# A selective scan whose last state column is copied by another engine

## The chip, the cores and the metric

The kernel runs on one core of one Trainium2 chip. The metric is the device time in microseconds of one execution; the time before is the median of three runs.

## The reference

A decoder layer over 4 sequences of 1024 tokens, width 512: a Mamba block, cross-attention to 64 context rows, a mixture-of-experts projection with low-rank experts, and a layer norm after each. What matters here is the scan of the Mamba block (d_inner 1024, 16 states):

```python
dA = jnp.exp(jnp.einsum('bld,dn->bldn', dt, A))
dBu = jnp.einsum('bld,bln,bld->bldn', dt, Bm, u_act)
def step(h, inputs):
    dA_t, dBu_t = inputs
    h = dA_t * h + dBu_t
    return (h, h)
_, hs = lax.scan(step, h0, (dA.transpose(1, 0, 2, 3), dBu.transpose(1, 0, 2, 3)))
y = jnp.einsum('lbdn,bln->bld', hs, Cm) + u_act * Dp
y = y * jax.nn.silu(z)
```

The block's output goes through a SwiGLU of width 2048. Cross-attention has 16 heads of 32, with a temperature for each head out of a small network that reads statistics of the scores.

## The kernel before

The work is cut into 8 chunks of 512 tokens; chunks 2b and 2b+1 are the halves of sequence b. An even chunk starts its scans from zero, an odd one from the state that the even one left. Channels lie on the 128 partitions, so 1024 channels make 8 blocks, taken in 4 pairs. One step of the scan is one pair and one of the 16 states over 512 tokens: 64 steps a chunk, 512 in all.

A step goes through three engines. GpSimd multiplies dt*u by the row of B (`times_b`, L1070) into one of three buffers `hb`. ScalarE makes the two decays with Exp into two PSUM banks (`decays`, L1127). VectorE runs two `tensor_tensor_scan` in place in `hb` (L1425), each of which frees its decay bank. GpSimd multiplies `hb` in place by the row of C (`times_c`, L1080). VectorE adds it to the sum in PSUM (L1435), which frees the buffer. GpSimd does the product by B of the next step ahead of the product by C of this one (AHEAD = 1), so its order is B(g+1), C(g), B(g+2), C(g+1). ScalarE's decays of step g+1 go into the banks that the scans of step g free.

In even chunks the last column of `hb` after the scan is the state that the odd chunk begins with. As the product by C overwrites `hb`, ScalarE first copies the two values of each partition into `state` (L1195), after the decays of the next step in its queue, and the product by C waits for it through the semaphore `st_saved` (L1078). In odd chunks there is neither copy nor wait. The odd chunk's first scan waits for all copies of its even chunk (L1419).

All the rest is dense work: the front of a chunk (norm, input projection, convolution; stream f), output projection (f), SwiGLU, norm, query (stream y), the statistics of attention (s), attention and experts (x, and w for the last chunk), the gates z and the softplus of dt (l). It's worked on beside the scan by TensorE, ScalarE and VectorE. The scan is stream m. The residual adds of GpSimd are L1100 and L1103, its product dt*u once per pair is L1090.

Every engine executes a list in fixed order. The lists come out of `schedule()`, a planner that runs when the kernel is built: `parts(u)` gives for each unit its costs by engine and what it waits for, and at each point an engine takes from the streams the unit that can begin first, with `LOOK` as a tolerance by stream; among units that are equally early the lower key wins. Stream m has key 0, l has 1; for the others the key is chunk + PHASE + (share done) / WORK. A unit that is late in reality holds up everything behind it in its engine's list. SyncE issues all loads in an order that follows the planned times too (`loads()`).

Of the kernel before, what the change touches and what calls it, by code (L numbers as in the profile page):

```python
# [7 lines left out]
BATCH, SEQ, DM, DI, NS, DTR, DFF = 4, 1024, 512, 1024, 16, 32, 2048  # L8
# [3 lines left out]
CH = 512  # L12
# [11 lines left out]
HB, AHEAD, BC = 3, 1, 2  # L24
# [7 lines left out]
PE, ACT_, DVE, POOL = "PE", "ACT", "DVE", "POOL"  # L32
# [22 lines left out]
def pair_of(n):  # L55
    return divmod(n, PAIRS)


def step_of(g):
    return divmod(g, STEPS)  # L60
# [104 lines left out]
def parts(u):  # L165


    kind, c, key = u[0], u[1], u[1:]
    i = u[2] if len(u) > 2 else None
    b, last, got = c // 2, TT - 1, []  # L170

    def part(eng, us, *after, takes=(), gives=(), name=None):
        got.append((eng, us, after, name, takes, gives))
# [25 lines left out]
    elif kind == "step":  # L199
        g, total = c * STEPS + i, CHUNKS * STEPS  # L200
# [3 lines left out]
        for n in (0, 1) if g == 0 else (g + 1,) if g + 1 < total else ():  # L204
            at = step_of(n)
            for jj in range(2):
                part(ACT_, 0.68, ("scan", *step_of(n - 1), jj), ("sp4", at[0], 2 * (at[1] // NS) + 1), name=("exp", *at, jj))
        if c % 2 == 0:
            part(ACT_, 0.2, ("scan", c, i, 1), name=("saved", c, i))
        if i % NS == 0:  # L210
            part(ACT_, 1.4, ("gate", *pair_of(g // NS - 1)), name=("yp", c, i // NS))
        for jj in range(2):
            part(DVE, 1.25, ("s1", c, i), ("exp", c, i, jj), name=("scan", c, i, jj))
        part(POOL, 2.35, ("scan", c, i, 1), ("saved", c, i), name=("s3", c, i))
    elif kind == "sum":
        part(DVE, 1.3, ("s3", c, i), ("yp", c, i // NS))
    elif kind == "gate":
# [143 lines left out]


SCAN_BANKS, DENSE_BANKS = (0, 1, 2, 3), (4, 5, 6, 7)
WORK = {"x": 1534.0, "w": 127.4, "s": 422.9, "y": 661.5, "f": 650.3}
PHASE = {
# [5 lines left out]
}  # L371


# [83 lines left out]
def schedule():  # L457
# [9 lines left out]
    for name, units in streams.items():  # L467
        for u in units:
            got = parts(u)
            todo[u] = len(got)  # L470
            pending.add(u)
            share[name] = share.get(name, {})
            share[name][u[1]] = share[name].get(u[1], 0.0) + sum(p[1] for p in got)
            key = 0 if name == "m" else 1 if name == "l" else u[1] + PHASE[name][u[1]] + share[name][u[1]] / WORK[name]
            by_eng = {}
            for n, p in enumerate(got):
                by_eng.setdefault(p[0], []).append((n, p))
                pending.add((u, n))
                if p[3]:
                    pending.add(p[3])  # L480
            for e, ps_ in by_eng.items():
                queue[e][name].append((u, ps_, key))
# [25 lines left out]
    while True:  # L508
        best = None
        for e in queue:  # L510
            names = (inside[e],) if inside[e] else streams
            mine = None
            for name in names:
                t = ready(e, name)
                if t is not None:
                    rank = (max(t, at[e] + LOOK[name]), queue[e][name][place[e][name][0]][2])
                    if mine is None or rank < mine[0]:
# [41 lines left out]
    return streams["m"], begun, {u: v[0] for u, v in done.items()}, order, taken  # L559


LOOK = {"m": 0.379, "l": 0.018, "x": 0.019, "w": 0.041, "s": 0.247, "y": 0.171, "f": 0.0}
MIXER, BEGUN, DONE, ORDER, DENSE_TAKES = schedule()


# [85 lines left out]
def decoder_layer(nc, A, out):  # L651
    f32 = mybir.dt.float32
    ALU = mybir.AluOpType
    ACT = mybir.ActivationFunctionType
    AX = mybir.AxisListType.X
    ctx = ExitStack()
    with ctx:
        def sb(name, shape):
            return ctx.enter_context(nc.sbuf_tensor(name, shape, f32))
# [43 lines left out]
        hb = sb("hb", [P, HB, 2, CH])  # L703
# [5 lines left out]
        state = sb("state", [P, JB, NS])  # L709
# [99 lines left out]
        s = type("Sems", (), S)  # L809
# [8 lines left out]
        def filled(eng, key):  # L818

            bank, n = USE[key]  # L820
            eng.wait_ge(full[bank], n + 1)
            return ps[:, bank]
# [21 lines left out]
        def emptied(eng, key):  # L844

            bank, n = USE[key]
            eng.wait_ge(free[bank], n + 1)
# [32 lines left out]
        def firsts_done(eng, n):  # L880

            at_least(eng, s.s1_ready, n)

        def summed(eng, n):

            eng.wait_ge(s.sum_done, n + 1)
# [162 lines left out]
        @block.gpsimd  # L1049
        def _(pool):  # L1050
            nc.gpsimd.memset(kbd[:, :, :, :], 0.0).then_inc(s.zeroed, 1)
            nc.gpsimd.memset(vbd[:, :, :], 0.0).then_inc(s.zeroed, 1)
            nc.gpsimd.memset(sta[:, :, :], 0.0).then_inc(s.zeroed, 1)
            nc.gpsimd.memset(eps_t[:, :], EPS).then_inc(s.zeroed, 1)
            nc.gpsimd.memset(ones_t[:, :], 1.0).then_inc(s.zeroed, 1)
            nc.gpsimd.memset(negs_t[:, :], -1.0).then_inc(s.zeroed, 1)
            nc.gpsimd.memset(zero3[:, :], 0.0).then_inc(s.zeroed, 1)
            nc.gpsimd.memset(t_w2[:, HID:P], 0.0).then_inc(s.zeroed, 1)

            TTn = nc.gpsimd.tensor_tensor  # L1060

            def times_b(n):
                c, k = step_of(n)
                if k % NS == 0:
                    pool.wait_ge(s.dtu_ready, n // NS + 1)
                pool.wait_ge(b_in[n % BC], 16 * (n // BC + 1))

                if n >= HB:
                    summed(pool, n - HB)
                TTn(hb[:, n % HB], dtu[:, :, :], bc[:, 0, n % BC].unsqueeze(1).broadcast_to([P, 2, CH]), ALU.mult  # L1070
                    ).then_inc(s.s1_ready, 1)

            def times_c(n):
                c, k = step_of(n)
                emptied(pool, ("da", c, k, 0))
                emptied(pool, ("da", c, k, 1))
                if c % 2 == 0:
                    pool.wait_ge(s.st_saved, (c // 2) * STEPS + k + 1)  # L1078
                pool.wait_ge(c_in[n % BC], 16 * (n // BC + 1))
                TTn(hb[:, n % HB], hb[:, n % HB], bc[:, 1, n % BC].unsqueeze(1).broadcast_to([P, 2, CH]), ALU.mult  # L1080
                    ).then_inc(s.s3_done, 1)

            for unit in ORDER[POOL]:
                kind, c = unit[0], unit[1]
                i = unit[2] if len(unit) > 2 else None
                if kind == "du":
                    emptied(pool, ("dt", c, 2 * i))
                    emptied(pool, ("dt", c, 2 * i + 1))
                    firsts_done(pool, c * STEPS + i * NS)
                    TTn(dtu[:, :, :], dt[:, i % 2], u[:, c % 2, 2 * i:2 * i + 2], ALU.mult).then_inc(s.dtu_ready, 1)  # L1090
                elif kind == "step":
                    g = c * STEPS + i
                    for n in range(AHEAD + 1) if g == 0 else (g + AHEAD,) if g + AHEAD < CHUNKS * STEPS else ():
                        times_b(n)
                    times_c(g)
                elif kind == "bo":
                    pool.wait_ge(s.const_in, 16 * CONSTS)
                    for c4 in range(KC):
                        filled(pool, ("tr", c, 0, c4))
                    TTn(res[:, c % 3, i], res[:, c % 3, i], bo_b[:, :], ALU.add).then_inc(s.bo_in, 1)  # L1100
                elif kind == "out":
                    emptied(pool, ("out", c, i))
                    TTn(res[:, c % 3, i], ht[:, i], res[:, c % 3, i], ALU.add).then_inc(s.res_in, 1)  # L1103
# [3 lines left out]
        def _(act):  # L1107
            A_ = nc.scalar.activation
# [20 lines left out]
            for unit in ORDER[ACT_]:  # L1129
                kind, c = unit[0], unit[1]  # L1130
                i = unit[2] if len(unit) > 2 else None
                b, half = divmod(c, 2)
# [36 lines left out]
                elif kind == "sp1":  # L1169
# [4 lines left out]
                    elif c or i:  # L1174
                        n, p = pair_of(c * PAIRS + i // 2 - 1)
# [10 lines left out]
                elif kind == "step":  # L1186
                    g = c * STEPS + i
                    for n in (0, 1) if g == 0 else (g + 1,) if g + 1 < CHUNKS * STEPS else ():
                        decays(*step_of(n))
                    p, n = divmod(i, NS)  # L1190
                    if half == 0:

                        emptied(act, ("da", c, i, 0))
                        emptied(act, ("da", c, i, 1))
                        A_(state[:, 2 * p:2 * p + 2, n], hb[:, g % HB, :, CH - 1], ACT.Copy).then_inc(s.st_saved, 1)  # L1195
                    if n == 0:
                        for jj in range(2):
                            key = ("yp", c, p, jj)
# [78 lines left out]
                elif kind == "e1":  # L1277
# [4 lines left out]
                    if wide1(c):  # L1282
                        n = 2 * i + hf
# [83 lines left out]
        def _(dve):  # L1367
# [14 lines left out]
            for unit in ORDER[DVE]:  # L1382
# [113 lines left out]
                elif kind in ("rstd", "xrstd"):  # L1496
# [3 lines left out]
                    else:  # L1500
                        dve.wait_ge(s.ln_sd, c + 1)
                    _, mean_var, sd = norm_of(x, c)
                    ch.link(V.reciprocal(sd[:, 1, :], sd[:, 0, :]))
                    V.scalar_tensor_tensor(sd[:, 2, :], mean_var[:, :, 0], -1.0, sd[:, 1, :], ALU.mult, ALU.mult
# [430 lines left out]
```

## Time and profile before

| what | value |
|---|---|
| median of three runs | 3673.43 us (3672.25 to 3678.02) |
| the profiled execution | 3670.03 us, span 3668.2 us |
| TensorE matmul busy | 3004.8 us, 82% |
| VectorE busy | 2788.1 us, 76% |
| GpSimd busy | 2532.7 us, 69% |
| ScalarE busy | 2141.0 us, 58% |
| chain that ended last | TensorE 18% of the span, VectorE 2%, ScalarE 2%, issue 1% |
| mean granted TensorE clock | 0.905 |

The span runs from the first to the last instruction. The chain that ended last is followed back from the end through what released each instruction; the shares named cover less than a quarter of the span. A wait is put down to the instruction that released it last. An engine's list can't be overtaken, so a wait at its head delays all that is behind it.

### The profile page before, as it was taken

The numbers are of one execution on the slowest core, as the hardware profiler recorded it, in microseconds if no ns is written. First come the engines' busy times: TensorE is split into PE (matmuls) and PEld (weight loads), VectorE is DVE, ScalarE is ACT, GpSimd is POOL, SyncE is SP. The second block draws the span as 40 slices with busy tenths as digits, with TensorE's granted clock in tenths as the row PEclk, the third lists the DMA queues.
The fourth block names the chain that finished last, engine by engine and source line by source line (L and its number), as shares of the span: only waits on it lengthen the run. The fifth ranks groups of instructions, "written<-read, shape, count | busy, mean of one in ns | idle before, by whom it ended". The sixth has DMA issues, their size and how long they took to land. (4 is left out here: it accounts for less than half of the span.)

```text
span 3668.2 us, 32780 instructions
## 1 busy us (share of the span) xinstructions
PE 3004.8 (82%) x8248; PEld 1452.7 (40%) x8248; DVE 2788.1 (76%) x3376; ACT 2141.0 (58%) x4823; POOL 2532.7 (69%) x1132
## 2 busy tenths in 40 slices
PE   6711389867986899899996899999998799999868
PEld 3200134333433444444443344444443344554444
DVE  3878889988888798879897788877898898322353
ACT  5544475567556775777558675667557756441332
POOL 0699969987988598876987677776798798300000
PEclk8855699978997999999997999999999799999979
DMA  4433445544554444554642444453555354212100
GB/s 158 122 115 127 147 142 192 171 137 153 177 169 124 133 150 141 174 166 133 203 167 93 154 135 141 157 172 135 159 175 170 123 175 143 101 42 88 39 1 23
DMA packets 225430, 497.91 MB, mean 136 GB/s; under 512 B 32348, under 2 KB 32732, under 8 KB 224988
## 3 DMA queue, kind: packets, MB, share of 16 engines
q1 hardware_dynamic: 225244, 495.82, 41.7%
q8 instruction: 70, 1.15, 0.1%
q14 instruction: 116, 0.95, 0.1%
HBM read 485.76 MB, written 9.96 MB: 135 GB/s over the span
## 5 line engine op out<-in xcount | busy, mean ns | idle before, releaser
L1080 POOL TENSOR_TENSOR hb<-hb,bc 128x1024 f32<-128x1024 f32 x512 | 1206.2, 2356 | 436.2 <-ACT state L1195 219.1
L1070 POOL TENSOR_TENSOR hb<-dtu,bc 128x1024 f32<-128x1024 f32 x512 | 1206.5, 2356 | 111.8 <-DVE ps L1435 107.0
L1127 ACT ACTIVATE ps<-dt,a_neg 128x512 f32<-128x512 f32 x1024 | 691.5, 690 | 687.2 <-DVE hb L1425 685.0
L1651 PE MATMUL ps<-fT,wden 128*128 128x512 f32 x2304 | 1036.2, 605 | 52.5 <-DVE dt L1413 7.5
L1425 DVE TENSOR_TENSOR_SCAN hb<-ps,hb 128x512 f32<-128x512 f32 x512 | 596.7, 1207 | 108.9 <-POOL hb L1070 96.6
L1651 PEld LDWEIGHTS ps<-fT,wden 128*128 128x128 f32 x2304 | 439.8, 194 | 600.1 <-issue 593.1
L1425 DVE TENSOR_TENSOR_SCAN hb<-ps,state,hb 128x512 f32<-128x512 f32 x512 | 627.2, 1266 | 65.5 <-POOL hb L1070 41.7
L1435 DVE TENSOR_TENSOR ps<-ps,hb 128x1024 f32<-128x1024 f32 x512 | 624.3, 1219 | 12.2 <-POOL hb L1080 11.8
L1651 PE MATMUL ps<-xnT,wmix 128*128 128x512 f32 x1024 | 456.7, 601 | 126.0 <-DMA wmix<-in_w_mix 113.4
L1741 PE MATMUL ps<-wden,hm 128*128 128x512 f32 x1024 | 456.2, 597 | 28.8 <-DVE res L1481 12.4
L1702 PE MATMUL ps<-wmix,u 128*128 128x512 f32 x512 | 241.2, 626 | 147.5 <-issue 82.0
L1651 PEld LDWEIGHTS ps<-xnT,wmix 128*128 128x128 f32 x1024 | 196.4, 193 | 374.9 <-issue 258.7
L1741 PEld LDWEIGHTS ps<-wden,hm 128*128 128x128 f32 x1024 | 191.8, 191 | 272.2 <-issue 224.9
L1702 PEld LDWEIGHTS ps<-wmix,u 128*128 128x128 f32 x512 | 100.7, 201 | 281.8 <-issue 209.2
L1100 POOL TENSOR_TENSOR res<-res,bo_b 128x512 f32<-128x512 f32 x32 | 39.8, 1276 | 243.5 <-PE ps L1754 243.5
L1777 PE MATMUL ps<-kbd,qT 128*128 128x256 f32 x512 | 150.0, 435 | 64.5 <-DVE se L1523 44.6
L1239 ACT ACTIVATE hm<-ps 128x512 f32<-128x512 f32 x128 | 76.2, 596 | 215.7 <-PE ps L1651 130.4
L1481 DVE TENSOR_TENSOR res<-ps,res 128x512 f32<-128x512 f32 x128 | 87.5, 683 | 112.8 <-PE ps L1741 112.4
L1393 DVE SCALAR_TENSOR_TENSOR ps<-stage,cols,ps 128x512 f32<-128x512 f32 x192 | 144.6, 753 | 32.0 <-ACT ps L1157 27.4
L1342 ACT ACTIVATE xw<-ps,nm,ftv 128x64 f32<-128x64 f32 x384 | 149.4, 416 | 6.0 <-PE ps L1777 5.8
L1465 DVE SCALAR_TENSOR_TENSOR hm<-hm,ps 128x512 f32<-128x512 f32 x128 | 86.8, 678 | 84.4 <-ACT hm L1239 83.6
L1777 PEld LDWEIGHTS ps<-kbd,qT 128*128 128x128 f32 x512 | 104.2, 215 | 105.7 <-DVE se L1523 54.5
(242 smaller groups left out, 3504.5 us busy)
## 6 DMA issues: line engine op xcount, KB each, us to landing
bc<-bc_dram SPq DMA_DIRECT2D x1024, 256.0 KB, 3.3
wden<-in_w SPq DMA_DIRECT2D x192, 512.0 KB, 3.9
wmix<-in_w_mix SPq DMA_DIRECT2D x128, 512.0 KB, 3.9
watt<-in_w_qof SPq DMA_DIRECT2D x26, 512.0 KB, 4.1
stage<-in_x SPq DMA_DIRECT2D x8, 1024.0 KB, 5.8
res<-in_x SPq DMA_DIRECT2D x8, 1024.0 KB, 6.6
wden<-in_w_qof SPq DMA_DIRECT2D x16, 512.0 KB, 4.2
out<-res SPq DMA_DIRECT2D x8, 1024.0 KB, 5.0
```

Of the source, the lines that this page charges most:

```text
L1070: TTn(hb[:, n % HB], dtu[:, :, :], bc[:, 0, n % BC].unsqueeze(1).broadcast_to([P, 2, CH]), ALU.mult).then_inc(s.s1_ready, 1)
L1080: TTn(hb[:, n % HB], hb[:, n % HB], bc[:, 1, n % BC].unsqueeze(1).broadcast_to([P, 2, CH]), ALU.mult).then_inc(s.s3_done, 1)
L1127: A_(dst, dt[:, p % 2, jj], ACT.Exp, scale=a_neg[:, j, n:n + 1]).then_inc(full_of(key), 1)
L1342: ins = A_(eb_of(c)[:, hh], bank[:, h], ACT.Exp, bias=nm2[:, TT * half + i, hh:hh + 1], scale=ftv[:, 0, hh:hh + 1], accum_out=den_of(c)[:, ...
L1393: ins = V.scalar_tensor_tensor(acc, up[:, i % 2, tap:tap + CH], conv_w[:, i, tap:tap + 1], acc, ALU.mult, ALU.add)
L1425: V.tensor_tensor_scan(hb[:, n % HB, jj], src, hb[:, n % HB, jj], first, ALU.mult, ALU.add).then_inc(free_of(key), 1)
L1435: V.tensor_tensor(ps[:, 2:4], ps[:, 2:4], hb[:, n % HB], ALU.add).then_inc(s.sum_done, 1)
L1481: V.tensor_tensor(res[:, c % 3, tt], src, res[:, c % 3, tt], ALU.add).then_inc(free_of(key), 1)
L1651: ins = M(dst, a, b, start=start and n == 0, stop=stop and n == len(pairs) - 1)
L1702: ins = M(ps[:, USE[key][0]], u[:, half, j, t * P:(t + 1) * P], wo[:, j % 2], start=j == 0, stop=j == JB - 1)
L1741: ins = M(dst, hm[:, f, tt * P:(tt + 1) * P], wi[:, (f % 2) * 512:(f % 2) * 512 + 512], start=f == 0, stop=f == FG - 1)
L1777: ins = M(dst[:, m * 256:(m + 1) * 256], qT[:, c4, T * P:(T + 1) * P], kbd[:, b % 2, c4], start=True, stop=True)
```

## The change

GpSimd copies the last column itself, right before the product by C in its own list, and then waits for its own copy by the same semaphore. ScalarE's copy is gone, with its two waits. In the planner the part of 0.2 on ScalarE is gone, the product by C costs 0.15 more in even chunks and no longer waits for the copy. All the constants of the planner's priorities, WORK, PHASE and LOOK, have other values, so that the order of the lists of all engines, and the order of the loads, may be another.

```diff
@@ parts(u), kind == "step"
-        if c % 2 == 0:
-            part(ACT_, 0.2, ("scan", c, i, 1), name=("saved", c, i))
...
-        part(POOL, 2.35, ("scan", c, i, 1), ("saved", c, i), name=("s3", c, i))
+        part(POOL, 2.35 + (0.15 if c % 2 == 0 else 0.0), ("scan", c, i, 1), name=("s3", c, i))
@@ planner constants
-WORK = {"x": 1534.0, "w": 127.4, "s": 422.9, "y": 661.5, "f": 650.3}
+WORK = {"x": 169.8, "w": 831.5, "s": 26.2, "y": 31.4, "f": 43.7}
 PHASE = {
-    "x": (34.753, 4.637, 32.716, 36.312, 63.287, 39.291, 57.599, 95.752),
-    "w": (12.607, 28.312, 24.365, -32.043, -13.09, 0.11, 30.675, 18.153),
-    "s": (0.314, -8.39, 7.942, 5.462, -10.774, -24.164, -52.826, -0.355),
-    "y": (38.588, 1.209, -24.936, -33.417, -23.064, -23.341, -23.392, -15.228),
-    "f": (15.256, -7.945, 2.695, 24.097, -13.326, -28.258, 38.233, -20.089),
+    "x": (36.744, 5.957, 40.05, 35.575, 68.382, 58.488, 60.427, 102.854),
+    "w": (7.884, 22.737, 33.738, -18.942, -11.063, 11.758, 36.876, 33.748),
+    "s": (8.781, -11.538, 8.696, -0.908, -19.87, -28.791, -53.763, -10.604),
+    "y": (47.653, 15.941, -14.86, -35.472, -20.046, -26.021, -8.484, 1.026),
+    "f": (20.176, 0.519, 12.645, 36.762, 1.801, -21.137, 44.543, -11.967),
 }
-LOOK = {"m": 0.379, "l": 0.018, "x": 0.019, "w": 0.041, "s": 0.247, "y": 0.171, "f": 0.0}
+LOOK = {"m": 0.384, "l": 0.043, "x": 0.022, "w": 0.044, "s": 0.245, "y": 0.237, "f": 0.0}
@@ GpSimd, times_c(n)
                 if c % 2 == 0:
+                    p, m = divmod(k, NS)
+                    nc.gpsimd.tensor_copy(state[:, 2 * p:2 * p + 2, m], hb[:, n % HB, :, CH - 1]).then_inc(s.st_saved, 1)
                     pool.wait_ge(s.st_saved, (c // 2) * STEPS + k + 1)
@@ ScalarE, kind == "step"
-                    if half == 0:
-
-                        emptied(act, ("da", c, i, 0))
-                        emptied(act, ("da", c, i, 1))
-                        A_(state[:, 2 * p:2 * p + 2, n], hb[:, g % HB, :, CH - 1], ACT.Copy).then_inc(s.st_saved, 1)
```

## Rows read from the trace of the kernel before

**Rows 1.** Busy us by stretch after the scan: PE, PEld, DVE, ACT, POOL, clock, DMA

```profile
3158.00:3450.00 292.00, 284.07 (x818) 141.48 (x816) 69.71 (x146) 93.24 (x297) 5.00 (x4) 0.98 0.23 78
```

**Rows 2.** The same view, chunks 0, 2, 4 and 6

```profile
98.90:434.00 335.10, 96.01 (x200) 37.56 (x198) 270.79 (x266) 167.38 (x297) 306.25 (x133) 0.64 0.39 121
795.00:1167.00 372.00, 312.57 (x735) 141.33 (x735) 319.80 (x350) 232.41 (x529) 315.73 (x140) 0.90 0.49 157
1560.00:1956.00 396.00, 371.86 (x978) 175.65 (x976) 332.94 (x409) 257.57 (x567) 321.26 (x145) 0.97 0.48 159
2370.00:2789.00 419.00, 385.51 (x1005) 181.50 (x1005) 343.29 (x418) 261.56 (x582) 316.76 (x143) 0.96 0.47 154
```

**Rows 3.** Chunk 0, one line's instructions and their waits: L1080, then L1425's wait

```profile
L1080 POOL TENSOR_TENSOR hb<-hb,bc x65: 2329/2347/2391, 98.9 to 432.4; 128x1024 f32<-128x1024 f32 x65
...
  ACT state L1195: 23.9, 5
...
  POOL hb L1070: 55.1, 47
```

**Rows 4.** L1080 in chunks 2 to 6: ns min/median/max, first, last start; waits: us, times

```profile
L1080 POOL TENSOR_TENSOR hb<-hb,bc x64: 2336/2354/2386, 799.8 to 1165.2; 128x1024 f32<-128x1024 f32 x64
...
  ACT state L1195: 33.5, 21
...
L1080 POOL TENSOR_TENSOR hb<-hb,bc x65: 2346/2356/2384, 1165.2 to 1558.1; 128x1024 f32<-128x1024 f32 x65
...
  issue: 63.4, 11
...
L1080 POOL TENSOR_TENSOR hb<-hb,bc x65: 2344/2355/2382, 1558.1 to 1954.4; 128x1024 f32<-128x1024 f32 x65
...
  ACT state L1195: 66.3, 24
...
L1080 POOL TENSOR_TENSOR hb<-hb,bc x65: 2334/2356/2400, 1954.4 to 2368.2; 128x1024 f32<-128x1024 f32 x65
...
L1080 POOL TENSOR_TENSOR hb<-hb,bc x64: 2340/2355/2377, 2368.2 to 2782.4; 128x1024 f32<-128x1024 f32 x64
...
  ACT state L1195: 95.4, 25
```

**Rows 5.** Timeline, a step of chunk 3: start us, us, what [idle before, releaser]

```profile
1235.66 2.46 DVE L1425 TENSOR_TENSOR_SCAN hb<-ps,state,hb 128x512 f32<-128x512 f32 x2
...
1238.25 2.36 POOL L1080 TENSOR_TENSOR hb<-hb,bc 128x1024 f32<-128x1024 f32 x1 [19.86 <-issue]
```

**Rows 6.** Timeline, a step of chunk 6 with a long wait

```profile
2526.97 2.34 DVE L1425 TENSOR_TENSOR_SCAN hb<-ps,hb 128x512 f32<-128x512 f32 x2 [1.64 <-ACT ps L1127]
...
2543.94 1.30 ACT L1127 ACTIVATE ps<-dt,a_neg 128x512 f32<-128x512 f32 x2
2545.16 0.20 ACT L1195 ACTIVATE state<-hb 128x2 f32<-128x2 f32 x1
...
2545.59 2.36 POOL L1080 TENSOR_TENSOR hb<-hb,bc 128x1024 f32<-128x1024 f32 x1 [13.09 <-ACT state L1195]
```

**Rows 7.** GpSimd: the timeline round L1090, and two groups (busy us, mean ns)

```profile
192.33 2.35 POOL L1080 TENSOR_TENSOR hb<-hb,bc 128x1024 f32<-128x1024 f32 x1
194.63 2.34 POOL L1090 TENSOR_TENSOR dtu<-dt,u 128x1024 f32<-128x1024 f32 x1
197.05 2.34 POOL L1070 TENSOR_TENSOR hb<-dtu,bc 128x1024 f32<-128x1024 f32 x1
...
L1057 POOL MEMSET zero<- 128x3 f32 x1 | 0.1, 101 | 0.0
...
L1100 POOL TENSOR_TENSOR res<-res,bo_b 128x512 f32<-128x512 f32 x32 | 39.8, 1276 | 243.5 <-PE ps L1754 243.5
```

**Rows 8.** Groups of VectorE: the scan with and without a carried state

```profile
L1425 DVE TENSOR_TENSOR_SCAN hb<-ps,hb 128x512 f32<-128x512 f32 x512 | 596.7, 1207 | 108.9 <-POOL hb L1070 96.6
L1425 DVE TENSOR_TENSOR_SCAN hb<-ps,state,hb 128x512 f32<-128x512 f32 x512 | 627.2, 1266 | 65.5 <-POOL hb L1070 41.7
```

## The prediction

> **What bounds the kernel now.** I read four views in this order: the chain that ended last (its shares stand in the table above, most of it TensorE's), busy time by stretch, the two GpSimd products by stretch, and single steps of the timeline. A step is one (pair, state) of the scan: GpSimd multiplies by B (L1070), ScalarE makes two exponentials (L1127), VectorE scans twice (L1425), GpSimd multiplies by C (L1080), VectorE adds (L1435). There are 512, 64 to a chunk, eight chunks. From 3158 us on GpSimd works 5 of 292 us, so the scan is over, while TensorE works 284 of them [rows 1]; with a span of 3668.2 us, some 510 us of dense work follow the scan. The end therefore moves only if the dense work starts sooner, which the scan governs, or if TensorE's idle time inside the scan shrinks.
>
> That idle time is 59 us of 372 in chunk 2, 24 of 396 in chunk 4, 33 of 419 in chunk 6, and 239 of 335 in chunk 0 [rows 2]. In chunk 0 there is no dense work yet, so whatever lengthens chunk 0 delays the first dense unit one for one. GpSimd is busy 306 of 335 us there, and VectorE waited 47 times, 55.1 us, for the product by B; GpSimd waited only 5 times, 23.9 us, for the copy [rows 2, 3]. So chunk 0 is paced by GpSimd. In chunks 2, 4 and 6 GpSimd waited for the copy 21, 24 and 25 times, 33.5, 66.3 and 95.4 us [rows 4]. That makes 70 of 192 steps and 195 us: the prize on the label.
>
> **How much of such a wait is the copy.** In an undisturbed odd step, where nothing is copied, the product by C starts 0.13 us after the second scan ends (1235.66 + 2.46 = 1238.12, then 1238.25) [rows 5]. In an even step two exponentials of the next step, which wait for the same scans, and then the copy stand in between: the second exponential takes 0.65 us (half of the 1.30 of two) and the copy 0.20, and with a hand-over like the odd step's 0.13 us once more about 0.95 us is lost against the odd step [rows 5, 6]. Long waits are of another kind. The longest shown, 13.09 us, has its scans over at 2529.31; ScalarE was in dense units ahead of this step and reached the copy at 2545.16 [rows 6]. After the change GpSimd would go on at about 2532.5, where it fell idle. But the next scans need exponentials from the same late ScalarE, so GpSimd does one product and the one by B behind it and then stands before the next product by C. What it gains is the product it has already done, at most 2.36 us, and not 13.
>
> **Part 1, the copy goes to GpSimd: its price.** It is paid in 256 steps. The trace has no GpSimd copy. Below, the nearest row is a memset of 128x3, 0.101 us; above, the fixed part of a two-input product, 2 x 1.276 - 2.355 = 0.197 us from its widths of 512 and 1024 [rows 4, 7]. To it comes the wait for its own semaphore (the new wait stays, now behind GpSimd's own copy). This one is in the trace: dtu's product is followed by the first product by B, which waits for it, and that starts at 197.05, 2.42 us after 194.63, where independent neighbours start 2.30 us apart (192.33 and 194.63) [rows 7]. That is 0.12 us. With 0.10 and 0.19 for the copy itself this makes 0.22 and 0.31. Behind the waiting product are queued the next product by B and the residual adds; VectorE waits for both. I take 0.25, nearer to the small memset, as two elements a partition are moved. It can't be nothing or a gain: it is one more instruction in a queue that starts each when the one before is nearly done.
>
> The Trainium skill (GPSIMD Engine Reference, the note that consecutive Pool instructions are not a barrier between Q7 cores) says that completion gates whatever waits on the semaphore, not the next instruction. This fits: 0.12 us more with a wait than without [rows 7]; by the page alone there is no figure for the sum.
>
> **Chunk 0.** 59 steps without a copy wait pay 0.25 us each, +15 us. The 5 that waited save 0.95 each, -5 us. Net +10 us, on the path because GpSimd paces the chunk and TensorE has nothing else; ends +8 (0.22) and +18 (0.31 and no saving, if those waits are the start-up's). The cover would be GpSimd's own idle time in the chunk, 335 - 306 = 29 us, 24 of which are these five waits, so there is hardly any.
>
> **Chunks 2, 4 and 6.** 70 waits, each worth 0.95 (the lag alone) to 2.36 us (one product). Most of the waits are short, so 1.2 is taken: 84 us. Price 192 x 0.25 = 48 us. Net 36 us of GpSimd's time. How much reaches the end? A control lies in the same trace: chunks 3 and 5 have the wait-free form throughout. From first to last product by C a step took 5.80 us in chunk 2 (365.4 over 63), 6.14 in chunk 3 (392.9 over 64), 6.19 in chunk 4 (396.3 over 64), 6.47 in chunk 5 (413.8 over 64) and 6.57 in chunk 6 (414.2 over 63) [rows 4]. Each odd chunk lies between its neighbours: 6.14 against their mean 6.00, and 6.47 against 6.38. The scans with a carried state cost 1.266 us in place of 1.207, 0.12 us a step [rows 8]; without it the odd ones would be at 6.02 and 6.35. So a chunk without the copy wait is no faster than one with it: in chunk 3 GpSimd stood 63.4 us in 11 waits before the product by C all the same [rows 4]. This speaks for a share near zero. On the other side, the odd chunks carry other dense units than the even ones, and TensorE still has 116 us idle in the three even chunks to take. Between these two I take a third: -12 us. Ends: 0, and two thirds, -24 us, with the waits at 1.2; at 2.36 each and all of it, 165 - 48 = 117 us, just TensorE's idle time, which no row makes likely.
>
> **Part 2, ScalarE loses 256 copies** of 0.20 us [rows 6]. Its dense units in even chunks start that much sooner: 192 x 0.20 = 38 us in chunks 2, 4 and 6, of which again only what was late counts. A quarter, -9 us; ends 0 and half, -18. In chunk 0 ScalarE has room, so nothing there.
>
> **Part 3, the planner.** It decides each engine's order, and with the step's costs (0.2 on ScalarE gone, 0.15 more on GpSimd, under my 0.25) all of its priorities change. A lower key goes first: chunk number plus PHASE, and over the chunk the share of its work by WORK. In chunk 3 the four dense streams y, s, f, x stood at -30.4, 8.5, 27.1 and 39.3 and stand at -32.5, 2.1, 39.8 and 38.6; in chunk 4 s moves ahead of f (-6.8 and -9.3 before, -15.9 and 5.8 after), in chunk 2 too; in chunk 1 y falls behind x. Most ranks stay, so most of the order should. The trace can't price another order. The nearest row is one stall that comes or goes with a unit's place, the 13.09 us of [rows 6]. I put it at zero, with ends of -20 and +20, one or two such stalls net.
>
> **Sum.** +10 - 12 - 9 + 0 = -11 us. The profiled execution took 3670.03 us (span 3668.2 and 1.8 around it), which gives 3659; the median of the three runs is 3.4 us above it, so against the median it is 3673.4 - 11 = 3662 us, 0.3% faster. A measurement of this kernel tells about 0.2% (7 us) from no change.
>
> **Rivals.** *Covered*: the share is zero as chunks 3 and 5 say, and ScalarE's relief is given back at the next dense wait. Then +10 and a few us of ScalarE's relief: 3673 to 3680, taken at 3676. For it: the step times of [rows 4]. Against: 70 waits that do vanish.
>
> *GpSimd becomes the bound (slower)*: the place is the row of products in even chunks. 122 steps of chunks 2, 4 and 6 did not wait for the copy and gain nothing; at 0.31 and half of them on VectorE's path they cost 122 x 0.31 / 2 = 19 us, with chunk 0 at +18, and the waits that go are replaced by waits for ScalarE's exponentials: 3673 + 37 = 3710, or 3673 + 15 + 10 = 3698 at 0.25. It decides from a price of 0.34 us a copy with the shares above (59 p - 5 + (192 p - 84) / 3 - 9 = 0), and at 0.25 as soon as ScalarE's relief is lost and under 10 / 36 of the net gain in the later chunks gets through. Against: VectorE waited for GpSimd's products by B in chunk 0 mostly [rows 3]. The Trainium skill (Perfetto Trace Analysis, Identifying the Most-Contended Engine) would have the engine with the highest occupancy relieved first; moving work from ScalarE (257.6 of 396 us in chunk 4) to GpSimd (321.3) goes the other way [rows 2], and by it this rival would hold.
>
> *The order*: the new sequence puts a dense unit that is late ahead of an exponential. One or two stalls of 13 us more: 3685 to 3695. The reverse, with two fewer and the whole two thirds: 3673 + 10 - 24 - 18 - 10 = 3631.
>
> **Chances.** Forecast 0.38 (3645 to 3666), the strong gain 0.07, covered 0.28, GpSimd's price 0.15, a worse order 0.12. Faster 0.44, same 0.27 (most of covered and the edge of the forecast), slower 0.29. The range takes in the strong gain's end and the slower rivals but for the last: 3630 to 3702.
>
> **What would show it.** The copy on GpSimd lasts 0.10 to 0.19 us and the product by C starts at least 0.22 us after the copy's start. In chunk 0 the step goes from near 5.2 to near 5.4 us and the next chunk's first product is 7 to 18 us later. GpSimd waits before the product by C in chunks 2, 4 and 6 fall from 195 us, but those named by VectorE's scans take much of their place; the steps there are 0.0 to 0.15 us shorter. The prediction is wrong if chunk 0 isn't longer, if a copy costs over 0.31 us, or if the chunks 4 and 6 change by more than 20 us each: then the order, and not the wait, made the result.

## The result

The changed kernel took 3693.4 us (median of four, 3687.05 to 3696.16) against 3672.84 us (median of four) for the kernel before: a ratio of 1.0052, 95% interval 1.0034 to 1.0069. It is some 19 us slower, where 11 us faster had been forecast. The time lies inside the range, on the other side of no change.

The profiled execution has a span of 3685.3 us. Busy time by stretch, chunks 0, 2, 4 and 6 of the kernel after, cut at the first product by C of each chunk (columns as in [rows 1]):

```profile
97.00:440.00 343.00, 93.08 (x192) 36.74 (x192) 271.02 (x263) 158.30 (x230) 315.47 (x197) 0.63 0.38 118
...
800.00:1169.00 369.00, 302.86 (x721) 137.59 (x720) 317.13 (x347) 224.74 (x450) 326.45 (x204) 0.90 0.51 158
...
1581.00:1984.00 403.00, 363.69 (x923) 169.49 (x921) 340.68 (x412) 252.61 (x517) 331.78 (x209) 0.94 0.49 158
...
2413.00:2782.00 369.00, 342.45 (x825) 152.51 (x824) 323.40 (x383) 219.88 (x405) 327.32 (x206) 0.97 0.52 167
```

Against [rows 2], GpSimd has 9 to 11 us more work in each and ScalarE less. Chunk 6 is some 55 us shorter and chunk 4 is 7 us longer (table below): that is no matter of a copy. The copy's own instructions and their waits in the kernel after, in chunks 2, 4 and 6 (they answer to the waits of [rows 4]):

```profile
L1077 POOL COPY state<-hb x63: 177/187/213, 804.5 to 1164.0; 128x2 f32<-128x2 f32 x63
...
  DVE hb L1420: 19.5, 7
...
  DVE hb L1420: 47.9, 14
...
  DVE hb L1420: 14.4, 5
```

The 195 us of waits for ScalarE's copy in these chunks are gone; 82 us of waits for the scans stand in their place. With the order of before (e1 below) it is 11.0 + 42.7 + 64.2 = 118 us.

How long each chunk lasts, in the profiled executions, from its first product by C to that of the next one, and the tail (us, worked out from first starts; chunk 7 lasts to the end of its last product by C, and the tail begins there). The experiments' names are explained below. Each row is a single execution and can lie up to 7 us from its kernel's median (e4: 3668.9 against 3676.1). Chunk 1 lies between 359.0 and 361.4 in all fourteen kernels, so 2 us in one chunk mean nothing by themselves.

| kernel | 0 | 1 | 2 | 3 | 4 | 5 | 6 | 7 | tail |
|---|---|---|---|---|---|---|---|---|---|
| before | 333.5 | 360.3 | 372.6 | 392.8 | 396.3 | 413.8 | 423.7 | 364.3 | 512.0 |
| after | 342.5 | 359.8 | 369.0 | 412.5 | 403.3 | 429.0 | 368.1 | 392.8 | 510.7 |
| e1, move only | 347.0 | 359.0 | 367.4 | 393.4 | 394.5 | 419.2 | 420.6 | 364.4 | 512.0 |
| e2, order only | 328.8 | 361.4 | 373.1 | 409.9 | 411.7 | 434.6 | 372.4 | 391.3 | 514.8 |
| e3, no copy, old order | 330.5 | 359.0 | 363.0 | 389.7 | 391.2 | 416.7 | 418.7 | 366.3 | 515.4 |
| e4, no copy, new order | 328.8 | 359.7 | 361.9 | 409.8 | 405.5 | 430.3 | 367.0 | 393.3 | 513.7 |

After has e1's longer chunk 0 and e2's pattern from chunk 3 on. So there are two parts, and they can be taken apart.

### The profile page after: what moved, and what is told of

Its sections match the earlier page's. It is cut to its first block, busy times and chain, and to the rows that moved or that the text cites. A ratio compares the mean times of both kernels' runs of the same rounds, so it can differ in the third digit from the quotient of the medians.

```text
span 3685.3 us, 32529 instructions
## 1 busy us (share of the span) xinstructions
PE 2989.2 (81%) x8248; PEld 1445.0 (39%) x8248; DVE 2791.8 (76%) x3376; ACT 2117.2 (57%) x4573; POOL 2575.0 (70%) x1388
## 3 DMA queue, kind: packets, MB, share of 16 engines
q1 hardware_dynamic: 225244, 495.82, 41.8%
## 4 chain that ended last, share of the span: by engine, by line
PE 58%; POOL 12%; ACT 11%; DVE 11%; issue 6%; DMA 1%; SPq 1%; POOLq 0%; DVEq 0%; ACTq 0%
PE ps L1646 39%; PE ps L1736 10%; POOL hb L1068 6%; POOL hb L1080 5%; DVE hb L1420 4%; ACT ps L1298 2%; PE ps L1697 2%; PE ps L1679 1%; PE ps L1772 1%; DVE ps L1430 1%; ACT xw L1337 1%; PE ps L1807 1%; ACT ps L1127 1%; PE ps L1840 1%; PE ps L1853 1%
## 5 line engine op out<-in xcount | busy, mean ns | idle before, releaser
L1080 POOL TENSOR_TENSOR hb<-hb,bc 128x1024 f32<-128x1024 f32 x512 | 1205.2, 2354 | 285.5 <-issue 251.1
L1420 DVE TENSOR_TENSOR_SCAN hb<-ps,hb 128x512 f32<-128x512 f32 x512 | 597.1, 1208 | 107.8 <-POOL hb L1068 101.1
L1090 POOL TENSOR_TENSOR dtu<-dt,u 128x1024 f32<-128x1024 f32 x32 | 75.3, 2354 | 94.6 <-DVE dt L1408 86.7
## 6 DMA issues: line engine op xcount, KB each, us to landing
wden<-in_w SPq DMA_DIRECT2D x192, 512.0 KB, 4.0
wmix<-in_w_mix SPq DMA_DIRECT2D x128, 512.0 KB, 4.1
watt<-in_w_qof SPq DMA_DIRECT2D x26, 512.0 KB, 4.5
wden<-in_w_qof SPq DMA_DIRECT2D x16, 512.0 KB, 4.2
```

The costliest lines, as they stand in the source:

```text
L1420: V.tensor_tensor_scan(hb[:, n % HB, jj], src, hb[:, n % HB, jj], first, ALU.mult, ALU.add).then_inc(free_of(key), 1)
```

## The experiments

All ratios are to the kernel before, run on the same chip beside them.

### The two parts of the change, one at a time

**e1** moves the copy and leaves the planner as it was:

```diff
+                    nc.gpsimd.tensor_copy(state[:, 2 * p:2 * p + 2, m], hb[:, n % HB, :, CH - 1]).then_inc(s.st_saved, 1)
...
-                        A_(state[:, 2 * p:2 * p + 2, n], hb[:, g % HB, :, CH - 1], ACT.Copy).then_inc(s.st_saved, 1)
```

> The copy goes to GpSimd and nothing else: every engine's order and the order of the loads are those of the kernel before. Theory A (the new order makes most of the loss): chunk 0 grows by 9 us as it did in the changed kernel (333.5 to 342.5 us from its first product by C to that of chunk 1), and later chunks give a part back, so 3672 to 3680 us. Theory B (the copy's price of 0.25 us on GpSimd makes the loss, in all 256 steps): 3688 to 3697 us, like the changed kernel.

Measured: 3675.96 us, ratio 1.0005 (0.9993 to 1.0017).

**e2** is the kernel after with those lines put back as they were: all planner constants and costs are the new ones, ScalarE copies.

> The order of the changed kernel on every engine, but ScalarE copies and GpSimd waits for it, as before. Theory A: 3680 to 3690 us, as chunks 3, 5 and 7 stay longer by the new order. Theory B: 3670 to 3677 us, no slower than the kernel before.

Measured: 3695.77 us, ratio 1.0068 (1.0050 to 1.0086), above both bands. Theory A holds, with a larger size than it gave: the new order alone is 23 us slower, and the move alone is within a few us of nothing on either order (+3.4 on the old one, 3693.4 - 3695.8 = -2.4 on the new one).

### What copy and wait are worth together

**e3** and **e4** have neither copy nor wait, in the old and the new order:

```diff
-                if c % 2 == 0:
-                    pool.wait_ge(s.st_saved, (c // 2) * STEPS + k + 1)
...
-                    if half and i == 0:
-                        dve.wait_ge(s.st_saved, (b + 1) * STEPS)
```

> The order of before, with no copy and no wait for one at all: the state that an odd chunk starts from is left at zero, so that part of the computation is left out. This is the most that taking the wait away can bring. If the wait is covered by late dense work, as chunks 3 and 5 of the kernel before suggested: 3665 to 3673 us. If 70 waits of about a microsecond reach the end by a third, as predicted: 3645 to 3660 us.

> The order of the changed kernel, with no copy and no wait (the carried state is left out and is zero). Against the changed kernel (3693 us) it leaves out only the 256 copies of 0.25 us on GpSimd. Theory A: 9 us less in chunk 0 and little elsewhere, 3680 to 3686 us. Theory B: 3670 us or less.

Measured: e3 3658.28 us, in the band of the predicted third, ratio 0.9962 (0.9947 to 0.9977); e4 3676.09 us, 1.0005 (0.9993 to 1.0017). So ScalarE's copy and the wait for it cost 14 us in the old order, and GpSimd's copy costs 17.7 us there (3675.96 - 3658.28) and 17.3 us in the new one (3693.4 - 3676.1). In the new order ScalarE's copy and wait cost 19.7 us (3695.8 - 3676.1). So the move is about even: it takes away 14 to 20 us and puts 17 to 18 in their place. e4 came in below what theory A expected, since GpSimd's copy costs 13.7 us in chunk 0 and not 9 (the new order by itself begins with a chunk 0 of 328.8 us), and is paid outside chunk 0 as well: 7.1 us of chunk 2 in the new order, 4.4 in the old. And e4 is slower than e3 by 17.8 us with no copy in either: the order's loss doesn't hang on the copy.

### The price of a GpSimd copy

The timeline of GpSimd in chunk 0 of the kernel after:

```profile
301.82 2.36 POOL L1068 TENSOR_TENSOR hb<-dtu,bc 128x1024 f32<-128x1024 f32 x1
304.12 0.18 POOL L1077 COPY state<-hb 128x2 f32<-128x2 f32 x1
304.39 2.35 POOL L1080 TENSOR_TENSOR hb<-hb,bc 128x1024 f32<-128x1024 f32 x1
306.70 2.34 POOL L1068 TENSOR_TENSOR hb<-dtu,bc 128x1024 f32<-128x1024 f32 x1
308.99 0.18 POOL L1077 COPY state<-hb 128x2 f32<-128x2 f32 x1
```

A step takes 308.99 - 304.12 = 4.87 us, where two products took 2 x 2.30 = 4.60 before [rows 7]: the price is 0.27 us, and in chunk 0 GpSimd has little idle time to hide it (e1: 18.5 us in 5 waits for the scans). **e6** doubles it, with a second copy and a second wait:

```diff
+                    nc.gpsimd.tensor_copy(state[:, 2 * p:2 * p + 2, m], hb[:, n % HB, :, CH - 1]).then_inc(s.st_saved, 1)
+                    pool.wait_ge(s.st_saved, 2 * ((c // 2) * STEPS + k) + 1)
```

> Order of before, copy on GpSimd, but done twice in each even step, each with its wait, so the price doubles from 0.25 to 0.5 us. If chunk 0 is bound by GpSimd, it grows by 64 x 0.25 = 16 us once more, from 347 to 363 us. If a GpSimd copy costs nothing behind dense work, the later chunks stay and the time is 3676 + 16 = 3692 us; if its price reaches the end by a third in chunks 2, 4 and 6 too, 192 x 0.25 / 3 = 16 us more, 3708 us.

Measured: 3709.07 us, ratio 1.0097 (1.0082 to 1.0112). The first product by C of chunk 0 and that of chunk 1, in e1 and then in e6:

```profile
L1082 POOL TENSOR_TENSOR hb<-hb,bc x65: 2337/2342/2362, 100.1 to 447.1; 128x1024 f32<-128x1024 f32 x65
```

```profile
L1084 POOL TENSOR_TENSOR hb<-hb,bc x65: 2340/2343/2368, 97.4 to 456.9; 128x1024 f32<-128x1024 f32 x65
```

347.0 and 359.5 us: +12.5 in chunk 0 (16 had been expected). Chunks 2, 4 and 6 grew by 9.6, 5.5 and 1.8 us, 17 of 192 x 0.25 = 48 us, so about a third of the price stays there. GpSimd is the bound in chunk 0, where 0.20 of 0.25 us a step come through. In the later chunks less comes through, and the less the busier TensorE is (308, 367 and 387 us in chunks 2, 4 and 6 of e1); that the one is the reason of the other isn't shown.

**e5** leaves chunk 0 with ScalarE and gives chunks 2, 4 and 6 to GpSimd:

```diff
                 if c % 2 == 0:
+                    if c:
+                        p, m = divmod(k, NS)
+                        nc.gpsimd.tensor_copy(state[:, 2 * p:2 * p + 2, m], hb[:, n % HB, :, CH - 1]).then_inc(s.st_saved, 1)
...
-                    if half == 0:
+                    if c == 0:
```

> Order of before. ScalarE copies in chunk 0, GpSimd in chunks 2, 4 and 6. The copy alone moved everywhere gave 3676 us. If its price is paid in chunk 0 alone (13 us there) and the later even chunks gain what they showed (5, 2 and 3 us shorter): 3660 to 3666 us. If the later chunks' gain was only the start-up's delay given back: 3671 to 3677 us.

Measured: 3665.41 us, ratio 0.9978 (0.9969 to 0.9987). Chunk 0 lasts 335.2 us, chunks 2, 4 and 6 last 368.3, 394.5 and 420.6: the gain in the later chunks is their own, 9 us over the three.

### Why long waits gave so little

The same stall in chunk 6, in the kernel before ([rows 6] shows its beginning) and in e1. GpSimd in the kernel before, and ScalarE's next exponentials:

```profile
2551.59 2.35 POOL L1080 TENSOR_TENSOR hb<-hb,bc 128x1024 f32<-128x1024 f32 x1 [1.34 <-ACT state L1195]
...
2556.22 2.35 POOL L1080 TENSOR_TENSOR hb<-hb,bc 128x1024 f32<-128x1024 f32 x1
...
2560.84 2.35 POOL L1080 TENSOR_TENSOR hb<-hb,bc 128x1024 f32<-128x1024 f32 x1
...
2557.76 0.69 ACT L1127 ACTIVATE ps<-dt,a_neg 128x512 f32<-128x512 f32 x1 [3.24 <-DVE hb L1425]
```

And in e1:

```profile
2541.77 2.36 POOL L1082 TENSOR_TENSOR hb<-hb,bc 128x1024 f32<-128x1024 f32 x1
2544.08 2.35 POOL L1070 TENSOR_TENSOR hb<-dtu,bc 128x1024 f32<-128x1024 f32 x1
2559.70 0.19 POOL L1079 COPY state<-hb 128x2 f32<-128x2 f32 x1 [13.27 <-DVE hb L1422]
2559.96 2.35 POOL L1082 TENSOR_TENSOR hb<-hb,bc 128x1024 f32<-128x1024 f32 x1
...
2565.44 2.36 POOL L1082 TENSOR_TENSOR hb<-hb,bc 128x1024 f32<-128x1024 f32 x1
...
2571.21 2.35 POOL L1082 TENSOR_TENSOR hb<-hb,bc 128x1024 f32<-128x1024 f32 x1
...
2555.91 1.29 ACT L1129 ACTIVATE ps<-dt,a_neg 128x512 f32<-128x512 f32 x2
...
2569.73 0.69 ACT L1129 ACTIVATE ps<-dt,a_neg 128x512 f32<-128x512 f32 x1 [3.36 <-DVE hb L1422]
```

Put e1's times back by 11.97 us, by which its ScalarE is later at this place (2555.91 against 2543.94 in [rows 6]). Four products by C in a row then start at 2529.80, 2547.99, 2553.47 and 2559.24, against 2545.59, 2551.59, 2556.22 and 2560.84 before. The lead of 15.8 us shrinks to 3.6, 2.8 and 1.6 us. The stall hasn't gone, it stands one step later, 13.27 us in place of 13.09, because the next scans wait for the exponentials of the same late ScalarE. And the first exponential after the stall for which ScalarE had to wait for a scan (3.24 us before, 3.36 in e1) comes at 2569.73 - 11.97 = 2557.76, to the hundredth where it was. So this long wait was worth next to nothing; the others weren't followed one by one.

### The lag without the price

**e7** leaves the copy with ScalarE, but puts it between the two exponentials of the next step:

```diff
                 for jj in range(2):
+                    if jj and c * STEPS + k > 0:
+                        save(c * STEPS + k - 1)
```

where `save` holds the lines that stood behind both exponentials before.

> Order of before, ScalarE copies as before, but between the first and the second exponential of the next step instead of behind both. The product by C is released about 0.65 us sooner, the second exponential starts 0.2 us later, and GpSimd pays nothing. If the 0.95 us lag of each of 75 waits is what the wait costs (the kernel without copy and wait was 14 us faster than before): 3660 to 3666 us. If the wait costs only where ScalarE is late with dense work, which this doesn't change: 3670 to 3674 us.

Measured: 3664.97 us, ratio 0.9977 (0.9969 to 0.9986). One hand-over in e7:

```profile
2523.86 0.69 ACT L1137 ACTIVATE ps<-dt,a_neg 128x512 f32<-128x512 f32 x1
2524.48 0.19 ACT L1125 ACTIVATE state<-hb 128x2 f32<-128x2 f32 x1
2524.58 0.67 ACT L1137 ACTIVATE ps<-dt,a_neg 128x512 f32<-128x512 f32 x1
...
2524.90 2.35 POOL L1080 TENSOR_TENSOR hb<-hb,bc 128x1024 f32<-128x1024 f32 x1 [6.67 <-ACT state L1125]
```

From the start of the first exponential to the product by C are 1.04 us; in the kernel before it was 2545.59 - 2543.94 = 1.65 [rows 6]. The long waits are there still (203 us in 69 waits over the whole kernel, 219 in 75 before), and the 0.6 us alone bring about half of what taking copy and wait away altogether brings (7.5 of 14.3 us). Chunks 2, 4 and 6 are 8 us shorter together, chunk 0 is as before (333.5 us). **e10** joins e7's place of the copy in chunk 0 with e5's GpSimd copies in the others.

> Order of before. In chunk 0 ScalarE copies between the two exponentials; in chunks 2, 4 and 6 GpSimd copies. The two halves gave 3665.0 (copy first everywhere) and 3665.4 us (ScalarE's late copy in chunk 0, GpSimd after). If chunk 0 has something left to gain from the earlier copy: 3660 to 3664 us; if GpSimd's 23.9 us of waits there are the start-up's: 3665 us.

Measured: 3665.27 us, ratio 0.9981 (0.9972 to 0.9989). Chunk 0 lasts 333.3 us, as in e7 and in the kernel before: the earlier copy has nothing to gain there. What e5 and e7 bring lies in chunks 2, 4 and 6 in both (9 and 8 us), so e10 has only one of the two gains, and their sum wasn't tried. e7, e5 and e10 beat both kernels by 0.2% and 0.7 to 0.8%; e7 is the simplest, as it moves one instruction within its own list.

### What in the planner makes the order slow

Four kernels change its inputs in groups. **e8** is the kernel before with the new PHASE and WORK, **e9** the kernel before with the new LOOK, **e12** the kernel after with the old PHASE and WORK. **e11** has GpSimd's copy and the new costs, with one value of LOOK changed from the old set:

```diff
-LOOK = {"m": 0.379, "l": 0.018, "x": 0.019, "w": 0.041, "s": 0.247, "y": 0.171, "f": 0.0}
+LOOK = {"m": 0.379, "l": 0.043, "x": 0.019, "w": 0.041, "s": 0.247, "y": 0.171, "f": 0.0}
```

> The kernel before with the new PHASE and WORK, the old LOOK and the old costs of a step. The lists of TensorE, ScalarE and VectorE change in places, GpSimd's does not. If the priorities carry the loss of the new order (23 us): 3690 to 3697 us. If LOOK and the step's costs do: 3668 to 3677 us.

> The kernel before with the new LOOK alone; costs, PHASE and WORK are the old ones and ScalarE copies. The planner's own plan then ends at 3740 us against 3707 for the kernel before, and 3717 for the changed kernel. If the chip follows the plan: about 30 us slower than before, 3695 to 3710 us. If a plan's end says nothing of the chip, 3673 to 3685 us.

> The copy on GpSimd and the new costs of a step, with PHASE, WORK and LOOK of before but for LOOK of stream l (0.043 in place of 0.018; with 0.018 the planner finds no complete order at all). Its plan ends at 3787 us, against 3717 for the changed kernel. If the chip follows the plan: about 70 us slower than the changed kernel, 3745 to 3770 us. If not: near 3693 us.

> The changed kernel with PHASE and WORK of before; costs and LOOK are the new ones. Its plan ends at 3717.1 us, the changed kernel's at 3716.8. With the old costs and LOOK the two sets of PHASE and WORK made no difference (3671.3 against 3672.5 us). So 3690 to 3697 us, as the changed kernel; 3676 us if the new PHASE and WORK were what hurts together with the new LOOK.

Measured, with the time at which each kernel's own plan ends:

| kernel | costs | LOOK | PHASE, WORK | plan ends | measured | ratio (95%) |
|---|---|---|---|---|---|---|
| before | old | old | old | 3706.6 | 3671 to 3673 | 1 |
| e8 | old | old | new | 3706.9 | 3671.33 | 0.9996 (0.9987 to 1.0005) |
| after | new | new | new | 3716.8 | 3693.4 | 1.0052 (1.0034 to 1.0069) |
| e12 | new | new | old | 3717.1 | 3692.54 | 1.0051 (1.0035 to 1.0066) |
| e9 | old | new | old | 3740.1 | 3699.42 | 1.0073 (1.0057 to 1.0088) |
| e11 | new | old but l | old | 3787.0 | 3766.49 | 1.0255 (1.0238 to 1.0272) |

The 45 new numbers of PHASE and WORK do nothing, in either set. The planner shows why: with the old costs and LOOK they give another unit at only 13 of TensorE's 1208 places, 19 of ScalarE's 1739, 22 of VectorE's 2248 and none of GpSimd's 608. The whole change gives another one at 483, 960, 1275 and 62 (compared place by place, so a unit put in early shifts those behind it). So this is no proof that such priorities never matter. LOOK alone costs 28 us (e9), and costs and LOOK together account for the whole loss of the order (e12). The chip follows the plans roughly: the two pairs of nearly equal plans are equal within their intervals, the pair at 3707 is the fastest and 3787 the slowest by far. Between 3717 and 3740 the intervals overlap, and the kernel after with ScalarE's copy (e2, plan 3716.8) is at 1.0068. With the new costs and the old PHASE and WORK, the old LOOK leads the planner into an order that it can't complete, and the LOOK chosen ends 10 us later than the plan it replaced. What the new costs do by themselves is thus not measured. e11 shows that this isn't a matter of the scan's pace alone: its scan is over sooner than that of the kernel after, but the dense work lies behind. Its last stretches:

```profile
3300.00:3500.00 200.00, 198.27 (x581) 99.14 (x580) 50.87 (x106) 58.13 (x175) 2.50 (x2) 0.98 0.19 64
3500.00:3761.00 261.00, 198.36 (x781) 119.28 (x779) 106.02 (x237) 89.20 (x211) 4.94 (x4) 0.88 0.05 19
```

Its tail after the last product by C is 607.9 us, against 512.0.

Where the new order loses is seen in e2. Chunks 3, 4, 5 and 7 in it (chunk 6 between):

```profile
1161.00:1571.00 410.00, 370.50 (x1111) 182.72 (x1111) 342.64 (x409) 269.13 (x634) 311.75 (x137) 0.96 0.46 146
1571.00:1982.00 411.00, 364.88 (x923) 169.20 (x921) 345.05 (x414) 262.33 (x589) 320.70 (x145) 0.94 0.48 155
1982.00:2417.00 435.00, 375.84 (x1146) 188.36 (x1147) 355.23 (x426) 296.24 (x723) 312.35 (x137) 0.92 0.43 138
2417.00:2790.00 373.00, 341.52 (x824) 151.65 (x823) 325.03 (x382) 227.45 (x468) 316.91 (x142) 0.97 0.51 165
2790.00:3181.00 391.00, 336.84 (x959) 165.98 (x958) 324.36 (x390) 247.92 (x607) 314.10 (x141) 0.92 0.44 141
```

And the same five chunks in the kernel before, cut in the same way:

```profile
1165.00:1558.00 393.00, 351.24 (x1020) 170.54 (x1019) 339.42 (x401) 257.12 (x579) 311.62 (x137) 0.96 0.48 152
1558.00:1954.00 396.00, 371.86 (x976) 175.51 (x976) 333.06 (x410) 257.46 (x563) 321.26 (x145) 0.97 0.48 159
1954.00:2368.00 414.00, 351.46 (x1021) 172.71 (x1020) 348.18 (x415) 287.17 (x718) 311.95 (x137) 0.93 0.45 143
2368.00:2792.00 424.00, 390.51 (x1020) 184.00 (x1019) 344.99 (x420) 263.60 (x587) 321.76 (x146) 0.96 0.46 152
2792.00:3156.00 364.00, 324.24 (x915) 158.90 (x914) 316.42 (x371) 229.84 (x553) 309.28 (x137) 0.92 0.45 148
```

TensorE's busy time stands behind the stretch's length, with its number of instructions. TensorE's idle time (length less its busy time) over these five is 39.5 + 46.1 + 59.2 + 31.5 + 54.2 = 230.5 us in e2 and 41.8 + 24.1 + 62.5 + 33.5 + 39.8 = 201.7 before: 29 us more, about the 27.7 us by which the two profiled spans differ. It stands in chunks 4 (+22) and 7 (+14). Work has moved between the chunks: TensorE has 91 instructions more in chunk 3 and 125 more in chunk 5, and 196 fewer in chunk 6. ScalarE's instructions of one line, the exponentials of the second attention pass with the reads of their sums, are a marker of it. In the kernel before, 224, 33, 213 and 49 of them lay in chunks 3 to 6; in the kernel after, in the same chunks:

```profile
1169.00:1581.00 412.00, 52.37 (x257) 0.95 0.46 145
1581.00:1984.00 403.00, 0.00 (x0) 0.94 0.49 158
1984.00:2413.00 429.00, 55.08 (x259) 0.93 0.43 140
2413.00:2782.00 369.00, 0.00 (x0) 0.97 0.52 167
```

This pass is now wholly in chunks 3 and 5, and what little of it lay in chunks 4 and 6 has left them (columns: start and end, length, ScalarE's busy time and count in that line, clock, DMA).

What TensorE waits for in chunk 4 can be read from the traces (what waited, for what: us in total, times, longest). Before, the only line of this view over 3 us:

```profile
PE ps L1754 <- DVE se L1523: 9.2, 1, 9.2
```

And in e2, all lines over 3 us:

```profile
PE ps L1775 <- DVE se L1521: 10.5, 2, 8.8
PE ps L1752 <- DVE se L1521: 7.9, 1, 7.9
PE ps L1649 <- DVE dt L1411: 6.8, 2, 6.1
PE ps L1752 <- ACT fT L1263: 4.4, 3, 2.0
PE ps L1752 <- DVE xw L1631: 4.0, 1, 4.0
```

Over the five chunks TensorE's waits that are put down to VectorE go from 104 to 138 us, those for ScalarE stay at 79, and those for a load go from 6 to 3. So the loss stands in waits for VectorE's results, and nothing in them points at the other order of the loads, which e2 has too. Which single displaced unit makes VectorE late in chunks 4 and 7 wasn't isolated.

## Why the prediction was wrong, point by point

- **The copy's price, 0.25 us (0.22 to 0.31):** right, 0.27 us. The copy itself takes 0.188 us, at the upper of the two rows it was bounded with (0.197, the fixed part of a two-input product), not near the memset's 0.101, as had been taken. The sum still came out because the product starts 0.08 us after the copy's end, as it did behind dtu's product (194.63 + 2.34 = 196.97, then 197.05 [rows 7]): of the 0.12 us taken for the wait, 0.04 are the overlap that it ends.
- **Chunk 0 is bound by GpSimd and grows by 10 us (8 to 18):** right, 13.5 us in e1 and 9.0 in the kernel after (13.7 against e2, which has its order).
- **Chunks 2, 4 and 6 give 12 us (0 to 24) and ScalarE's lost copies 9 us more:** they can only be measured together. e1's three chunks are 5.2 + 1.8 + 3.1 = 10.1 us shorter, against 21 in the sum. The two terms together were twice too large. How the 10 us are shared between them isn't shown, as no run relieves ScalarE alone. The reasoning on long waits, that only about one product is gained, held for the one stall that was followed.
- **The odd chunks as a control (share near zero):** they pointed too low. The short lag did reach the end: 7.5 us in e7 for 0.6 us a step, 14 us in e3. An odd chunk carries other dense work (TensorE has 1020 instructions in chunk 3 and 734 in chunk 2), so its equal pace didn't show that the even one's wait was free.
- **The move as a whole, -11 us:** it was +3.4 on the old order, its interval just reaching 3 us under zero. So the sign of this part, faster, wasn't borne out either. In the profiled executions chunk 0 took 3.5 us more than forecast, the later even chunks gave 11 us less, and chunk 5 was 5.4 us longer, which no term had.
- **The order, zero with ends of -20 and +20:** this step failed. It is +23 us, outside its ends and more than all other terms. "Most ranks stay, so most of the order should" looked at PHASE and WORK, the part of the planner's input that turned out to do nothing, and passed over LOOK (28 us by itself in e9) and gave the step's costs no effect of their own. And its size was taken from one stall, while the new lists have another unit at 483 of TensorE's 1208 places. What the runs showed in its place is 29 us more idle time of TensorE in chunks 3 to 7, with its waits for VectorE 34 us longer. That the time still lies in the range is due to the range's width and to no step of the sum.
- **The rivals:** the one on the order named the right part of the change and the time (3685 to 3695 us), at a chance of 0.12; its mechanism, a late unit ahead of an exponential, isn't shown. GpSimd as the bound explains chunk 0 and not the result. The Trainium skill (Perfetto Trace Analysis, Identifying the Most-Contended Engine) says to optimize first the engine with the highest occupancy. The traces agree for chunk 0, where GpSimd is the busiest (306 of 335 us [rows 2]) and the chunk grows by 13.5 us in e1 and by 12.5 more in e6. In chunk 4 it isn't the busiest (321 us, VectorE 333 [rows 2]), so by that rule the rival needn't have held there, and over the whole kernel moving the copy to GpSimd was neutral (1.0005).
- **What would show it:** the last sentence of the prediction, that chunks 4 and 6 changing by over 20 us would mean that the order made the result, was the right test, though only one half of it was met: chunk 6 changed by 56 us, chunk 4 by 7.

## What to carry to other kernels

When a diff changes a scheduler's costs along with an instruction, it is two changes, and the reordering can be the larger one: time each alone before either is believed. If the scheduler's own plan got longer, as here by 10 us, expect no gain from it: no kernel here with a longer plan was faster for its order, though 10 us of plan cost 19 and 33 us cost 28. And a wait for an engine that is itself late can stay when it's no longer named, as the one followed here did: look at when the next thing of that engine is needed, and try first to move the small instruction forward in its own list, which here brought 7.5 us and no price that shows.

## What the runs showed of the hardware

A GpSimd copy of 128x2 float32 took 0.177 to 0.213 us, 0.188 in the median; with the wait for its own semaphore the next product started 0.27 us after it and a second copy 0.25 us after the first. By the times of the product at two widths (2 x 1.276 - 2.355 = 0.197 us [rows 4, 7]) that is an instruction's fixed part on GpSimd, an estimate; ScalarE's copy of the same shape took 0.190 us.
